# Row statistics of the second normalisation taken in the attention stage, gelu output weighed by the vector engine

## The reference

```
h = patches(x) -> layernorm -> W + b, joined with text rows (table[id] + position)
h = h + attention(layernorm(h))              # 12 heads of 16, q = k = v, causal
h = h + ffn(layernorm(h))
ffn(x)        = bitlinear(gelu(bitlinear(x, w1, g1)), w2, g2)     # 192 -> 768 -> 192
bitlinear(x)  : xn = x * rsqrt(mean(x*x) + 1e-6) * g
                scale = 127 / max(|xn|) over the row;  xq = round(xn * scale) / scale
                xq @ ternary(w).T
layernorm(x)  = (x - mean) / sqrt(var + 1e-5)
```

## Time and profile before

| | us |
|---|---|
| median of three runs | 1896.07 (1895.81 to 1897.97) |
| profiled execution, its own time | 1889.4 |
| its span | 1887.7 |
| attention stage in it | about 190 to 1360 |
| FFN stage in it | 1360 to 1887.7 |

### The profile page before, as it was taken

The page is one execution under the profiler, slowest core; times in us unless marked ns, Lnnn a source line. Parts: engine busy times, 40 slices in busy tenths (PEclk is TensorE's granted clock), DMA queues, the critical chain, the costliest instruction groups (busy, mean ns, idle before and its releaser), DMA issues.

```text
span 1887.7 us, 50796 instructions
## 1 busy us (share of the span) xinstructions
PE 1579.8 (84%) x16574; PEld 1297.6 (69%) x16574; DVE 1364.8 (72%) x3151; ACT 1283.7 (68%) x1958; POOL 1089.7 (58%) x1503
## 2 busy tenths in 40 slices
PE   0539999999999999999999999999466666666666
PEld 0427788888888888888888888887345555555555
DVE  3636676767767676767676767676389999999996
ACT  1226666766767676767676666665288888888887
POOL 5035555555555555555555555554177777777775
PEclk9869999999999999999999999999666666666665
DMA  8674666665657565756565666660000000000000
GB/s 102 141 127 59 95 87 96 86 99 83 103 79 104 83 99 83 99 88 94 89 94 91 91 93 88 94 87 25 17 16 21 21 21 22 22 22 22 22 22 26
DMA packets 159967, 132.96 MB, mean 70 GB/s; under 512 B 32558, under 2 KB 151040, under 8 KB 159808
## 3 DMA queue, kind: packets, MB, share of 16 engines
q1 hardware_dynamic: 159168, 131.00, 44.4%
q0 software_dynamic: 768, 1.57, 0.5%
HBM read 118.32 MB, written 11.91 MB: 69 GB/s over the span
## 4 chain that ended last, share of the span: by engine, by line
PE 66%; DVE 15%; issue 7%; SPq 3%; ACT 3%; DMA 3%; POOL 1%; DVEq 1%; ACTq 0%; POOLq 0%
PE ps L1092 20%; PE ps L1176 8%; PE ps L1259 7%; PE ps L1250 7%; PE ps L1206 4%; DVE ff_st L860 4%; PE ps L1238 3%; PE ps L1232 3%; PE ps L1211 3%; PE ps L1336 2%; PE ps L1355 2%; DVE xpix L841 2%; PE ps L1167 2%; DVE xpix L853 1%; PE ps L1157 1%
## 5 line engine op out<-in xcount | busy, mean ns | idle before, releaser
L1092 PE MATMUL ps<-w_eff,pix 118*112 118x193 f32 (+1 forms) x2048 | 408.4, 337 | 25.0 <-ACT pix L909 24.3
L927 ACT ACTIVATE probs<-ps,isw 116x688 f32<-116x688 f32 x384 | 299.2, 831 | 171.6 <-PE ps L1238 171.6
L527 POOL TENSOR_TENSOR xpix<-probs,g_b 112x192 f32<-112x192 f32 (+1 forms) x512 | 296.5, 609 | 109.1 <-ACT probs L1044 99.7
L741 DVE TENSOR_REDUCE nmax<-ps 116x12 bf16<-116x1344 f32 (+2 forms) x192 | 299.6, 1560 | 80.2 <-PE ps L1211 77.7
L452 POOL TENSOR_TENSOR xsq<-xsq 118x784 f32<-118x784 f32 (+2 forms) x192 | 221.8, 1155 | 218.5 <-ACT xsq L920 208.4
L1092 PEld LDWEIGHTS ps<-w_eff,pix 118*112 118x112 f32 (+1 forms) x2048 | 309.8, 167 | 52.4 <-issue 18.9
L472 POOL TENSOR_SCALAR_AFFINE_SELECT probs<-probs 116x464 f32<-116x464 f32 x384 | 268.2, 717 | 46.5 <-ACT probs L927 31.0
L909 ACT ACTIVATE pix<-xpix 118x896 f32<-118x896 f32 (+1 forms) x128 | 198.4, 1552 | 104.9 <-DMA xpix<-in_x 56.0
L457 POOL TENSOR_TENSOR front_st<-front_st,expo 128x2 f32<-128x2 f32 x64 | 45.0, 703 | 235.2 <-DVE front_st L693 221.2
L1336 PE MATMUL ps<-w1t,xpix 96*112 96x384 f16 (+1 forms) x512 | 160.7, 488 | 14.6 <-ACT xpix L1035 13.3
L685 DVE TENSOR_SCALAR front_st<-ps 112x1 f32<-112x1 f32 (+1 forms) x128 | 18.3, 151 | 213.8 <-PE ps L1157 202.4
(11 more groups left out here) (161 smaller groups left out, 3363.3 us busy)
## 6 DMA issues: line engine op xcount, KB each, us to landing
xpix<-in_x SPq DMA_DIRECT2D x192, 196.0 KB
xpix<-in_x SPq DMA_DIRECT2D x192, 195.1 KB
rden<-den_rows SPq DMA_DIRECT2D x256, 85.5 KB, 2.1
out<-xpix SPq DMA_DIRECT2D x64, 87.0 KB
out<-xpix SPq DMA_DIRECT2D x64, 84.0 KB
xpix<-in_x SPq DMA_DIRECT2D x128, 34.1 KB
xpix<-in_x SPq DMA_DIRECT2D x128, 34.0 KB
den<-o_sb SPq DMA_DIRECT2D x256, 2.7 KB
```

The costliest lines, as they stand in the source:

```text
L527: last = nc.gpsimd.tensor_tensor(v2[0:P, b, tile, cols], gel[0:P, b, tile, cols], g2_b[0:P, cols], ALU.mult)
L741: V.tensor_reduce(dst, src, AX_X, ALU.max, negate=True).then_inc(s_mx, 1)
L927: A(probs[0:TB, g, 2 * e:2 * e + 2, :], ps[0:TB, 4 + 2 * e:6 + 2 * e, 0:SK], ACT.Exp, scale=isw[0:TB, 7:8]).then_inc(s_p, 1)
L1092: last = MM(ps_tok[tile][0:P, :], src, w_eff[0:HI, o, :], start=(o == 0), stop=(o == OFFS - 1))
```

## The change

1. The mean, variance, centring and peak of the second normalisation are taken in the attention stage: a new function `measure(n - 1)` is the last thing in DVE's `step_images`. POOL takes its root in `row_roots`. Results for all images are kept in small arrays. `v1` now shares its memory with `tok_t`.
2. Between the stages five DVE instructions on 128x128 numbers turn roots and peaks into the first quantiser's scales for all images.
3. In the FFN stage DVE centres again from the kept mean (`centre`), weighs both tiles of the gelu output itself (`weigh`, one instruction of 768 columns per tile), and computes only the second quantiser's scales. ACT's quantiser waits per tile. POOL keeps only the roots (`gelu_roots`).
4. The orders of TensorE and ACT in the FFN stage stay as they were.

```
+            def row_roots(m):
+                pool.wait_ge(s_var2, m + 1)
+                nc.gpsimd.tensor_tensor(rms[:, bass.ds(m * 2, 2)], ln_st[:, 32:34], expo[:, 0:2],
+                                        ALU.pow).then_inc(s_rms, 1)
...
                     clear_later(n, 2)
+                if prev:
+                    row_roots(n - 2)
                 if newest:
                     add_squares(n + 3)
...
-                        for lo in range(0, HIDDEN, HIDDEN // 4):
-                            cols = slice(lo, lo + HIDDEN // 4)
-                            last = nc.gpsimd.tensor_tensor(v2[0:P, b, tile, cols], gel[0:P, b, tile, cols],
-                                                           g2_b[0:P, cols], ALU.mult)
-                        last.then_inc(f_v2, 1)
...
+            def gelu_roots(n, b):
+                pool.wait_ge(f_ssq, 2 * n + 2)
+                apart(pool)
+                nc.gpsimd.tensor_scalar(ff_st[:, b, 18:20], gel_sum[:, b, :], EPS_RMS, None,
+                                        ALU.add).then_inc(f_var, 1)
+                pool.wait_ge(f_var, n + 1)
+                nc.gpsimd.tensor_tensor(ff_st[:, b, 20:22], ff_st[:, b, 18:20], expo[:, 0:2],
+                                        ALU.pow).then_inc(f_r1, 1)
...
+            def measure(n):
+                def chain(ins, k):
+                    ins.then_inc(s_mean2, 1)
+                    dve.wait_ge(s_mean2, n * 3 + k)
+                dve.wait_ge(s_h2, n + 1)
+                apart(dve)
+                for tile, P in enumerate((TA, TB)):
+                    last = V.bn_stats(ln_st[0:P, 20 + 6 * tile:26 + 6 * tile], h_all[0:P, hcols(n, tile)])
+                chain(last, 1)
+                apart(dve)
+                for tile, P in enumerate((TA, TB)):
+                    last = V.bn_aggr(ln_st[0:P, 34 + 2 * tile:36 + 2 * tile], ln_st[0:P, 20 + 6 * tile:26 + 6 * tile])
+                chain(last, 2)
+                after(dve, s_rms, n)
+                V.tensor_scalar(ln_st[:, 32:34], ln_st[:, 35:38:2], 1.0 + EPS_RMS,
+                                EPS_LN * EPS_RMS, ALU.mult, ALU.add).then_inc(s_var2, 1)
+                V.tensor_copy(mean2[:, bass.ds(n * 2, 2)], ln_st[:, 34:38:2])
+                for tile, P in enumerate((TA, TB)):
+                    last = V.scalar_tensor_tensor(v1[0:P, tile, :], h_all[0:P, hcols(n, tile)],
+                                                  ln_st[0:P, 34 + 2 * tile:35 + 2 * tile], g1_b[0:P, :],
+                                                  ALU.subtract, ALU.mult)
+                chain(last, 3)
+                for tile, P in enumerate((TA, TB)):
+                    last = V.tensor_reduce(peak[0:P, bass.ds(n * 2 + tile, 1)], v1[0:P, tile, :], AX_X, ALU.max,
+                                           apply_absolute_value=True)
+                last.then_inc(s_peak, 1)
...
                     maxima(n + 1, 2)
+                if prev:
+                    measure(n - 1)
...
+            dve.wait_ge(s_peak, IMAGES)
+            dve.wait_ge(s_rms, IMAGES)
+            link(V.tensor_tensor(peak[:, :], rms[:, :], peak[:, :], ALU.mult))
+            link(V.tensor_scalar(peak[:, :], peak[:, :], 1e-5, None, ALU.max))
+            link(V.reciprocal(inv_peak[:, :], peak[:, :]))
+            V.tensor_scalar(step1[:, :], peak[:, :], isw[:, 4:5], None, ALU.mult)
+            link(V.scalar_tensor_tensor(scale1[:, :], inv_peak[:, :], 127.0, rms[:, :], ALU.mult, ALU.mult))
...
+            def quantise_first(n):
+                dve.wait_ge(f_v1, n + 1)
+                after(dve, f_t1, n)
+                for tile, P in enumerate((TA, TB)):
+                    ins = V.tensor_scalar(q1[0:P, tile, :], v1[0:P, tile, :], scale1[0:P, bass.ds(n * 2 + tile, 1)],
+                                          MAGIC16, ALU.mult, ALU.add)
+                ins.then_inc(f_q1, 1)
...
+            def weigh(n, b):
+                for tile, P in ((0, TA), (1, TB)):
+                    after(dve, f_q2[tile], n - 1)
+                    dve.wait_ge(f_g, 2 * n + tile + 1)
+                    V.tensor_tensor(v2[0:P, b, tile, :], gel[0:P, b, tile, :], g2_b[0:P, :],
+                                    ALU.mult).then_inc(f_v2[tile], 1)
...
+            def ffn_step(i, b, new=True, mid=True, last_=True, fresh=True):
+                if new:
+                    centre(i + 1)
+                if last_:
+                    final(i - 3, 1 - b)
+                if fresh:
+                    weigh(i, b)
                 if mid:
...
+                    peaks(i - 1, 1 - b)
+                if new:
+                    quantise_first(i + 1)
                 if mid:
...
+                    second_scales(i - 1, 1 - b)
...
+            def quantise(n, b):
+                act.wait_ge(f_sc, n + 1)
+                after(act, f_t2, n)
+                for tile, P in enumerate((TA, TB)):
+                    act.wait_ge(f_v2[tile], n + 1)
+                    A(q2[0:P, tile, :], v2[0:P, b, tile, :], ACT.Copy, bias=MAGIC16,
+                      scale=ff_st[0:P, b, 38 + tile:39 + tile]).then_inc(f_q2[tile], 1)
```

More of the change, by code:

```diff
@@ L240, in build @@
         f_sc = sem("quantiser_scales_ready")
[L241 to L242 removed]
+        f_v2 = [sem(f"gelu_weighted{i}") for i in range(2)]
+        f_q2 = [sem(f"second_quantised{i}") for i in range(2)]
         f_t2 = sem("second_transposed")
@@ L509, in _ @@
             step_images(IMAGES - 1, 0, None, newer=False, newest=False)
[L511 to L524, removed]
-                        for lo in range(0, HIDDEN, HIDDEN // 4):
-                            cols = slice(lo, lo + HIDDEN // 4)
-                            last = nc.gpsimd.tensor_tensor(v2[0:P, b, tile, cols], gel[0:P, b, tile, cols],
-                                                           g2_b[0:P, cols], ALU.mult)
-                        last.then_inc(f_v2, 1)
[L530 to L537, removed]
+            row_roots(IMAGES - 2)
+            row_roots(IMAGES - 1)
+            def gelu_roots(n, b):
[6 more added lines that the diff above has]
+                                        ALU.pow).then_inc(f_r1, 1)
+            gelu_roots(0, 0)
+            gelu_roots(1, 1)
+            with pool.Fori(1, PAIRS) as t:
                 for b in range(2):
[L539 to L542, removed]
+                    gelu_roots(2 * t + b, b)
         @block.vector
@@ L569, in _ @@
             step(V.memset(nmax[:, :, :], 0.0))
+            for filled in (mean2, rms, peak):
+                step(V.memset(filled[:, :], 1.0))
             dve.wait_ge(s_const, 32)
@@ new lines, in centre @@
+            def centre(n):
+                after(dve, f_q1, n)
+                for tile, P in enumerate((TA, TB)):
+                    ins = V.scalar_tensor_tensor(v1[0:P, tile, :], h_all[0:P, hcols(n, tile)],
+                                                 mean2[0:P, bass.ds(n * 2 + tile, 1)], g1_b[0:P, :],
+                                                 ALU.subtract, ALU.mult)
+                ins.then_inc(f_v1, 1)
+            def quantise_first(n):
[5 more added lines that the diff above has]
+                ins.then_inc(f_q1, 1)
@@ new lines, in final @@
+            def final(n, b):
+                dve.wait_ge(f_m2, n + 1)
+                after(dve, f_out, 32 * n)
+                for tile, P in enumerate((TA, TB)):
+                    end = V.scalar_tensor_tensor(y[0:P, tile, :], ps[0:P, 1, tile * 256:tile * 256 + DIM],
+                                                 ff_st[0:P, b, 42 + tile:43 + tile], h_all[0:P, hcols(n, tile)],
+                                                 ALU.mult, ALU.add)
+                end.then_inc(f_y, 1)
+            def weigh(n, b):
[4 more added lines that the diff above has]
+                                    ALU.mult).then_inc(f_v2[tile], 1)
@@ L1037, in ffn_step @@
                 if mid:
-                    quantise(i, b, 0)
-                    quantise(i, b, 1)
+                    quantise(j, 1 - b)
                 if new:
-                    after(act, f_v2, 2 * m - 2)
+                    for tile in range(2):
+                        after(act, f_v2[tile], m - 1)
                     for tile, P in enumerate((TA, TB)):
```

140 lines of the change are left out of this document (53 added, 87 removed).

## The result

The changed kernel takes 1993.11 us (median of 4 runs, 1991.68 to 1999.69). The kernel before, run beside it, takes 1897.02 (4 runs, 1895.81 to 1900.55). The ratio is 1.051, with a 95% interval of 1.0483 to 1.0538: slower. The prediction was 1988, within 1945 to 2012. The profiled execution took 1993.21, its span is 1991.5.

The account below looks back on a forecast made before the run. DVE, 92% busy, was taken to set the FFN stage's pace before; afterwards a closed chain of waits, 9.42 us a step. FFN stage +90.6 and border +1.2 gave +91.8 on 1896.07: 1988 us, range 1945 to 2012.

Parts of the forecast that it names:

- The circle: FFN step: first quantiser, TensorE, gelu, DVE's weighing, peaks, next first quantiser in a closed chain; 9.42 us against 8.0, chance 0.72.
- a slow one: FFN step with TensorE at its low clock: 5.23 us from first quantiser to end of ffn_first, against 4.23.
- two gaps: In the FFN step: from ffn_first to the gelu, 0.03 us; DVE's wait for its peaks, 0.13 us.
- 5.05: FFN step: us from the end of the first quantiser to the end of ffn_first, taken between 5.23 and 4.23.
- longer pauses make more slow steps: FFN stage: TensorE stands still longer between bursts, so 5.05 us was taken, nearer 5.23 than 4.23.
- Border: Between the stages, statistics to end of the first image's first quantiser: 5.5 us against 4.27, so +1.2, bounds 0 and +3.
- first steps: Start of the FFN stage: first step 7.0 us without peaks, next two 8.7 each without ffn_second.
- the tail: End of the FFN stage, from the last first quantiser to the end: left at 24.1 us, give or take 3.
- the cover: Attention stage: DVE's wait for TensorE's L1157, 2.85 or 3.26 us, just hides measure's 2.75 us; cost 0.
- Its bound of 12 us: Attention stage: if measure ran over by 0.2 us beyond the margin, it would cost 62 x 0.2 = 12 us.
- My reading of the margin: Attention stage: thin slack behind the front, L730 ending at 909.78 and TensorE's dependent L1250 starting at 909.93.
- The waits named as signs: FFN profile: DVE's largest idle ahead of L888, ended by ACT's gelu, about 1.5 us an image; gelus 9.4 us apart.

Follow-up runs that it names:

- q1_ahead: Changed kernel with the next image's first quantiser moved ahead of DVE's weighing: 1855.21 us, ratio 0.9836 to the kernel before.
- weigh_last: Changed kernel with DVE's FFN order centre, first quantiser, peaks, final, second scales, weighing last: 1827.05 us, ratio 0.964 to the kernel before.
- peaks_behind: Changed kernel with the peaks moved behind the next image's first quantiser on DVE: 1874.8 us, ratio 0.9926 to the kernel before.
- extra_dve: Changed kernel with three unread bn_stats added on DVE in each full FFN step: 1988.75 us, ratio 1.0539 to the kernel before.
- both pairs: Kernel before and changed kernel, profiled, then both unchanged and profiled again: ratio 1.051 first, 1.0529 in the repeat.
- measure_only: Kernel before with only measure and row_roots added in the attention stage, results unused: 1898.33 us, ratio 1.005 to the kernel before.
- measure_more: Kernel of measure_only with its peak reductions done three times, 1.07 us more: 1918.02 us, ratio 1.0105 to the kernel before.
- Pool_weighs: Changed kernel with weighing back on POOL, DVE's order centre, final, peaks, first quantiser, second scales: 1828.94 us, ratio 0.9655 to the kernel before.

## Why the prediction was right

**The circle.** Named and placed rightly: q1_ahead and weigh_last open it and the loss is gone, peaks_behind shortens it by 1.87 us, where the terms taken out measure 2.09, extra_dve loads DVE beside it and nothing happens. Its length was predicted as 9.42 and is 9.54. In the step shown, against the prediction's terms for a slow one (9.60): q1 to the end of ffn_first 5.22 for 5.23, to the gelu 0.13 for 0.03, gelu 0.90, hand-over 0.04 for 0.10, weighing 0.87 for 0.86, peaks 1.80, DVE's wait for its own result 0.30 for 0.13, q1 0.55. Mis-sized were two gaps, 0.10 and 0.17 too short. The second was read between L860 and the small L866, but ahead of q1 DVE waits for its own peaks 0.29 us each time.

**The clock.** I took 5.05 for q1 to the end of ffn_first. The mean over the 60 steps is 4.91 (4.19 to 5.23), hardly more than before (4.86). Steps below 4.4 are 12 of 60, and were 10 of 60 before. TensorE's granted clock in the stage is 0.69 after 0.66, although its wait ahead of q1's turn grew from 2.35 to 4.0 us. My argument that longer pauses make more slow steps was too dear by 60 x 0.14 = 8 us, and by luck hid that the other terms, the two gaps above all, were 60 x 0.26 = 16 us too short. The rule of the Trainium skill ("TensorE: Matmul & The Clock Gate", section "HAM oscillation — how this bites in real kernels"), by which each burst starts cold, I had turned into 1999 us by holding every burst cold to the end of ffn_first. The traces bear out the cold starts: the granted clock is 0.50 when the turn of q1 starts in all 60 steps, where before it was in 40 of 60. They do not bear out that reading of the rule: in the 12 short steps the clock rises before ffn_first is through, and the mean is 4.91, not 5.23.

**Border and first steps.** 6.16 us for 5.5: one of the four instructions of 128 columns that I had at some 0.3 is the reciprocal, 0.95. Behind q1(0) it is 621.0 for 613.7; 60 steps of 0.12 are these 7.3. The first steps came out 0.8 us shorter in all and the tail 0.6 us longer (24.7), so these two misses cancel.

**measure.** Predicted as hidden. The wait for TensorE ahead of the front, 600 to 1000, before and after:

```profile
DVE front_st L685 <- PE ps L1157: 68.2, 22, 3.3
```

```profile
DVE front_st L690 <- PE ps L1200: 8.3, 21, 0.6
```

It is down from 3.1 us a step to 0.4, so the cover was nearly used up, as predicted. The median step of the attention stage is the same with and without it in both pairs. In whole stages its cost could not be resolved: measure_only says 6 to 13 us in all, of which 4.5 are in the FFN stage and its border, while whole attention stages of one kernel differ by 13 us between executions. Its bound of 12 us holds. My reading of the margin was wrong in size and in place: measure_more pays 0.16 of 1.07, and what TensorE then waits for is POOL's clearing (0.34 us a step), not L730.

**The sum.** +91.8 predicted; +103.8 between the two profiled executions, +96.1 between the medians. The 1988 is nearer the 1993 than its terms deserve: they were about 8 us short of the 100 that both pairs of profiles give for the FFN stage and its border, and the other few lie in differences between executions ahead of it. That part of the agreement is luck.

The waits named as signs are there: L888 has DVE's largest idle time, 1.5 us an image, with L1086 as releaser; gelus are 9.5 us apart; L871 takes 0.55. DVE is busy 67% in the FFN stage, not the 75% that I named. That figure did not follow from my own terms: 6.8 us of work and gaps an image, over 9.42, is 72%, and the gaps don't count as busy.

Left open: why the attention stage differs between executions, and where measure_only's 2 to 8 us outside the FFN stage and its border lie.

## What to carry to other kernels

Before an instruction moves to an engine with time to spare, write down what it waits for and what stands behind it in that engine's order: the busy shares say only what could be reached. If it waits for a result that hangs on an instruction queued behind it in the same list, its whole way round becomes the length of a step; put producers for other engines first and the instruction with the wait last (same instructions, a ratio of 0.964 instead of 1.051 to the kernel before). When all engines fall below 75% at once, as here, look in the list of waits for such a circle; an extra load beside it tests it.

## What the runs showed of the hardware beyond that

Short DVE instructions take longer while POOL is streaming. By shape in 1450 to 1850, the kernel before (POOL busy 74%):

```profile
L877 DVE TENSOR_SCALAR xpix<-xpix,ff_st 112x192 f16<-112x192 f32 x50 | 28.4, 568 | 1.8
...
L867 DVE TENSOR_SCALAR ff_st<-ff_st 128x4 f32<-128x4 f32 x50 | 24.2, 484 | 1.7
```

and the changed kernel (POOL 12%):

```profile
L888 DVE TENSOR_TENSOR xpix<-probs,g_b 112x768 f32<-112x768 f32 x42 | 40.2, 958 | 55.0 <-ACT probs L1086 55.0
...
L871 DVE TENSOR_SCALAR xpix<-tok_t,scale 112x192 f16<-112x192 f32 x42 | 13.7, 326 | 12.2 <-DVE ff_st L894 12.2
...
L904 DVE TENSOR_SCALAR ff_st<-ff_st 128x2 f32<-128x2 f32 x42 | 7.1, 169 | 1.4
```

The first quantiser goes from 568 to 326 ns, the small scale from 484 to 169, while the reductions of 768 columns keep their 0.94 us. (The scale has two columns instead of four, but at the border at 1363.34, with POOL at rest, the one of four columns takes 0.17 us too.) Pool_weighs has the changed kernel's instructions on DVE and the weighing back on POOL, which is busy 77% there. Its first quantiser, the same instruction as L871:

```profile
L884 DVE TENSOR_SCALAR xpix<-tok_t,scale 112x192 f16<-112x192 f32 x52 | 53.5, 1029 | 15.0 <-DVE ff_st L907 15.0
```

It takes 1029 ns, against 320 in weigh_last, where DVE weighs and POOL is busy 14%; the reductions keep 0.94 us. So the cause is POOL's weighing. How much it adds in an execution of the usual length is shown by the kernel before alone.

The products of 768 columns take 958 ns singly and 1.83 us for two, so the prediction's 0.86 for the second was right. A reciprocal of 128 columns takes 0.95 us, more than three times its neighbour of the same size (0.28).
